# A graph layer with a routed mixture of experts: 104 expert units moved, in pairs, in between the steps over the adjacency matrix

## The reference, cut to what matters

```python
def gnn(z, dist, W, B):                      # z: 8192 x 128, dist (adj): 8192 x 8192
    msg = z @ W + B
    sens = exp(-(1.0 / dist - 1.0) ** 2 / (2 * 0.5 * 0.5))
    weights = where(dist < 1.0, sens, 0.0)
    return weights @ msg

def ffn(x, gate_w, gate_b, w1, b1, w2, b2, gamma, beta):      # 16 experts, 2 for each row
    topk_vals, topk_idx = top_k(x @ gate_w + gate_b, 2)
    topk_w = softmax(topk_vals)
    h = relu(einsum("bsh,ehf->bsef", x, w1) + b1)             # 128 -> 256
    expert_out = einsum("bsef,efh->bseh", h, w2) + b2         # 256 -> 128
    y = x + sum(topk_w[..., None] * take(expert_out, topk_idx))
    return layernorm(y) * gamma + beta

x = x + gnn(layernorm(x), adj, W, B)
x = x + ffn(layernorm(x))
```

## Time and profile before

| what | value |
|---|---|
| median of 3 runs | 1704.23 us (1702.94 to 1705.1) |
| profiled execution, span from first to last instruction | 1823.2 us |
| adjacency loop in it | about 25 to 1433 us |
| tail in it | about 1433 to 1823 us |
| busy: TensorE, ScalarE, VectorE, GpSimd | 1624.7, 1565.7, 1499.7, 463.6 us |

### The profile page before, as it was taken

How to read it: one execution, slowest core, us unless ns; L and a number is a source line. 1 busy time by engine, 2 the same in 40 slices (tenths; PEclk the granted TensorE clock), 3 DMA queues, 4 the chain that set the end, 5 groups by cost and what they waited for, 6 DMA issues and landing times.

```text
span 1823.2 us, 24195 instructions
## 1 busy us (share of the span) xinstructions
PE 1624.7 (89%) x8178; PEld 1073.6 (59%) x8178; DVE 1499.7 (82%) x2298; ACT 1565.7 (86%) x1502; POOL 463.6 (25%) x342
## 2 busy tenths in 40 slices
PE   4999999999999999999999999999999987384720
PEld 3666666666666666666666656666666786373620
DVE  7999998989899999999999989999998443153464
ACT  5899999999999999999999999999999664253531
POOL 0001223131314040407132231313140213535342
PEclk9999999999999999999999999999999999696765
DMA  9559867676767676776776676787673244343431
GB/s 313 158 160 290 235 199 215 195 217 193 214 195 212 196 212 198 220 213 202 210 202 209 199 210 199 209 247 208 202 206 121 80 124 143 87 141 97 129 110 50
DMA packets 216792, 338.22 MB, mean 186 GB/s; under 512 B 18080, under 2 KB 74144, under 8 KB 216544
## 3 DMA queue, kind: packets, MB, share of 16 engines
q1 hardware_dynamic: 208368, 319.62, 59.8%
q0 software_dynamic: 8304, 17.06, 3.1%
HBM read 303.07 MB, written 33.55 MB: 185 GB/s over the span
## 4 chain that ended last, share of the span: by engine, by line
PE 84%; DVE 6%; another core or an unknown queue 5%; issue 3%; ACT 1%; DMA 1%; DVEq 0%; SPq 0%; ACTq 0%
PE acc L1118 48%; PE tp L1137 24%; PE tp L1164 4%; PE tp L1192 3%; PE acc L1192 2%; DVE chunk L654 1%; PE tp L1153 1%; DVE stats L666 1%; DVE chunk L660 1%; DVE chunk L1004 1%; PE misc L1094 1%; ACT chunk L613 1%; DVE msg L729 1%; DMA xs<-in_x_dram 1%
## 5 line engine op out<-in xcount | busy, mean ns | idle before, releaser
L1118 PE MATMUL acc<-wT,msg 128*128 128x512 f32 x2048 | 976.0, 599 | 0.0
L527 ACT ACTIVATE wT<-tp 128x1024 f32<-128x1024 f32 x512 | 761.0, 1674 | 14.0 <-PE tp L1137 12.4
L521 ACT ACTIVATE chunk<-chunk 128x2048 f32<-128x2048 f32 x256 | 655.3, 2560 | 0.1
L660 DVE SCALAR_TENSOR_TENSOR chunk<-chunk 128x2048 f32<-128x2048 f32 x256 | 584.8, 2284 | 54.7 <-ACT chunk L521 54.1
L1137 PEld LDWEIGHTS tp<-ident,chunk 128*128 128x128 f32 x4096 | 478.7, 141 | 223.2 <-issue 221.5
L654 DVE SCALAR_TENSOR_TENSOR chunk<-chunk 128x2048 f32<-128x2048 f32 x256 | 583.5, 2280 | 1.9 <-DMA chunk<-in_adj_dram 1.9
L1137 PE MATMUL tp<-ident,chunk 128*128 128x128 f32 x4096 | 534.3, 274 | 0.0
L516 ACT ACTIVATE chunk<-chunk 128x4096 f32<-128x4096 f32 x118 | 511.0, 4331 | 0.0
L1118 PEld LDWEIGHTS acc<-wT,msg 128*128 128x128 f32 x2048 | 349.1, 190 | 258.3 <-issue 245.8
L457 POOL TENSOR_TENSOR pool_carrier<-pool_carrier 1x1 f32<-1x1 f32 x32 | 43.7, 1365 | 951.5 <-DVE row_now L845 825.9
L476 POOL DMA_INDIRECT rows_in<-y,row_now x128 | 216.7, 1693 | 40.4 <-issue 40.4
(11 more groups left out here) (121 smaller groups left out, 794.7 us busy)
## 6 DMA issues: line engine op xcount, KB each, us to landing
chunk<-in_adj_dram SPq DMA_DIRECT2D x256, 1024.0 KB, 5.4
chunk<-rows_in SPq DMA_DIRECT2D x118, 64.0 KB
rows_out<-chunk SPq DMA_DIRECT2D x59, 128.0 KB
chunk<-rows_in SPq DMA_DIRECT2D x35, 128.0 KB
rows_out<-chunk SPq DMA_DIRECT2D x17, 256.0 KB
y_kept<-y SPq DMA_DIRECT2D x16, 256.0 KB, 6.1
chunk<-y_kept SPq DMA_DIRECT2D x16, 256.0 KB
out_dram<-chunk SPq DMA_DIRECT2D x16, 256.0 KB
```

The costliest lines, as they stand in the source:

```text
L521: act.activation(slot(c), slot(c), ACT.Exp, scale=-1.0).then_inc(inverted, 1)
L527: act.activation(wT[:, (g * PPG + m) % WSLOTS, :], tp[(g * PPG + m) % TSLOTS][:, :], ACT.Exp, scale=-2.0).then_inc(weighted, 1)
L660: dve.scalar_tensor_tensor(out=slot(c), in0=slot(c), scalar=2.0, in1=slot(c), op0=ALU.subtract, op1=ALU.mult).then_inc(squared, 1)
L1118: ins = pe.matmul(acc[:, :], msg[:, n, :], wT[:, (g * PPG + m) % WSLOTS, k * ROWS:(k + 1) * ROWS], start=(n == 0), stop=(n == 2 * PPG - 1))
```

## The change

- Units are always 128 rows; batches are 7, 5, 3 and 1 groups with 72, 55, 39 and 23 units, 189 in all.
- 52 pairs of units (all 36 pairs of the first batch and 16 of the second) run inside the loop in slots behind steps 279, 283, ... A slot does three things for three different pairs, one after the other on TensorE: second layer of pair p - 2, first layer of pair p - 1, transposes of pair p. A slot takes a place in the rotation of the three `tp` banks, so the steps behind it find one bank fewer. ScalarE's part stands behind `weigh` and `invert` at m % 4 = 3, VectorE's (`add_pair_bias`) ahead of the mask of the next step, SyncE loads rows 7 steps ahead of the slot and the first layers one step ahead of it.
- First layers live in DRAM (`first_layers`) until the loop's end; SyncE loads them by pair, and all of them at step 503.
- Tables are made one slot a step from the 26th step of the group after the batch's last.
- Groups 0 to 4 are gathered and combined in the loop (`gather_early`, `early_slot`, from steps 436, 461, 471, 493, 503), wholly on VectorE and GpSimd; these gathers stand on GpSimd between a group's `guess` and its scatter.
- The tail has 85 units, 11 combines starting at iterations 16, 27, 51, 62, 73, 84, 95, 106, 117, 128 and 139 of 152, the gate of group 15 one slot an iteration, the third batch's table at iterations 0 to 10 (its first slots still in the loop) and the fourth's at 26 to 42.

```diff
-    BATCHES = (7, 5, 4)
-    TILES = (1, 2, 1)
...
+    BATCHES = (7, 5, 3, 1)
...
+    UNITS = [K * n * TB + E - 1 for n in BATCHES]
+    UNITS[0] += UNITS[0] % 2
...
+    SLOT_EVERY = 4
+    PAIR_FIRST = [0, UNITS[0] // 2]
+    SECOND_PAIRS = 16
+    NP = PAIR_FIRST[1] + SECOND_PAIRS
+    NE = 2 * NP
+    AT_STEP = [(FIRST[b + 1] + 1) * PPG + 23 for b in range(2)]
+    FIRST_STEP = AT_STEP[0]
+    GRID_OF = [p if p < PAIR_FIRST[1] else (AT_STEP[1] - AT_STEP[0]) // SLOT_EVERY + p - PAIR_FIRST[1] for p in range(NP)]
+    assert GRID_OF[PAIR_FIRST[1]] >= PAIR_FIRST[1] + 2
+    GRID = sorted({t + d for t in GRID_OF for d in range(3)})
+    SLOT_STEP = [FIRST_STEP + SLOT_EVERY * t for t in GRID]
...
+    SLOT_AFTER = {step: n for n, step in enumerate(SLOT_STEP)}
...
+    def place(step):
+        return step + sum(at < step for at in SLOT_STEP)
...
+        COMBINE_FROM = (16, 51, 0, 0)
...
+            for g in range(FIRST[b], FIRST[b + 1]):
+                if g in LATE:
+                    at = max(COMBINE_FROM[b], TAIL0[b + 1] + 8)
+                    starts[g] = max(at, starts[g - 1] + COMBINE_LONG) if starts else at
+        LAST = starts[GROUPS - 1] + COMBINE_LONG + 2
...
+    EARLY_AT = (436, 461, 471, 493, 503)
+    EARLY_GATE = (12, 13, 13, 14, 14)
+    EARLY = len(EARLY_AT)
+    EARLY_SLOTS = 8
...
+            def load_pair(p):
+                if p in PAIR_FIRST:
+                    batch_there(pair_batch(p))
+                if p in PAIR_FIRST or p % PAIRS_AT_ONCE == 0:
+                    take_rows(2 * p, 2 * pairs_until(p))
+                if p >= 3:
+                    sp.wait_ge(turned, slot_place(TURN_SLOT[p - 3]) + 1)
+                for h in range(2):
+                    sp.dma_start(pair_in[:, p % 3, h, :],
+                                 rows_in[bass.ds(unit_rows[2 * p + h], P), :]).then_inc(pair_rows[p % 3], 16)
...
+            def load_pair_weights(p):
...
+                    sp.wait_ge(weighted, WSLOTS + slot_place(HIDDEN_SLOT[p - 2]) + 1)
+                for h in range(2):
+                    sp.dma_start(pair_w[:, p % 2, h, :],
+                                 first_layers[bass.ds(unit_experts[2 * p + h], 1), :, :].rearrange("a p f -> p (a f)")
+                                 ).then_inc(pair_weights[p % 2], 16)
...
+                    if s == SLOT_STEP[OUT_SLOT[p]] + 3:
+                        store_pair(p)
+                    if s == SLOT_STEP[TURN_SLOT[p]] - 7:
+                        load_pair(p)
+                    if s == SLOT_STEP[TURN_SLOT[p]] - 1:
+                        load_pair_weights(p)
+                for h in range(EARLY):
+                    if s == EARLY_AT[h] - 6:
+                        load_early(h)
+                    if s == EARLY_AT[h] + 9:
+                        store_early(h)
...
+            def gather_early(h):
+                last_carried()
+                if h == 0:
+                    results_there(0)
+                    pool.wait_ge(idx_ready, 1)
+                else:
+                    pool.wait_ge(early_free, h)
+                carry()
+                gather(h, 0, early_back, early_rows)
...
+                if h == 0 or g == FIRST[b]:
+                    results_there(b)
+                    pool.wait_ge(idx_ready, b + 1)
+                if h >= BACK:
+                    pool.wait_ge(back_free, h - BACK + 1)
+                carry()
...
+            for g in range(GROUPS):
+                guess(g)
+                for h in range(EARLY):
+                    if EARLY_GATE[h] == g:
+                        gather_early(h)
+                        guess_early(h)
+                if g == GROUPS - 1:
+                    for late in range(EARLY, FIRST[1]):
+                        gather_late(late)
+                scatter(g)
+            for g in range(FIRST[1], GROUPS):
+                gather_late(g)
...
+                act.wait_ge(turned, place(s) + 1)
+                act.wait_ge(added, s + 1)
+                act.activation(wT[:, s % WSLOTS, :], tp[place(s) % TSLOTS][:, :], ACT.Exp, scale=-2.0).then_inc(weighted, 1)
...
+            def pair_slot(n):
+                hid, turned_rows, _ = pair_bank(n)
+                act.wait_ge(turned, slot_place(n) + 1)
+                if n in TURN_SLOT:
+                    ins = act.activation(pair_rT[:, :], turned_rows, ACT.Copy)
+                if n in HIDDEN_SLOT:
+                    p = HIDDEN_SLOT.index(n)
+                    for h in range(2):
+                        for t in range(FT):
+                            i = h * FT + t
+                            ins = act.activation(pair_hT[:, i * P:(i + 1) * P], hid[:, i * P:(i + 1) * P], ACT.Relu,
+                                                 bias=pair_w[:, p % 2, h, F + t:F + t + 1])
+                if n not in TURN_SLOT and n not in HIDDEN_SLOT:
+                    ins = act.activation(act_carrier[:, :], eps[0:1, :], ACT.Copy)
+                ins.then_inc(weighted, 1)
...
+            def add_pair_bias(n):
...
+                if p >= 2:
+                    dve.wait_ge(pair_stored[p % 2], p // 2 * 16)
+                dve.wait_ge(weighted, WSLOTS + slot_place(n) + 1)
+                for h in range(2):
+                    ins = dve.tensor_tensor(pair_out[:, p % 2, h, :], pair_bank(n)[2][:, h * D:(h + 1) * D],
+                                            blobs[:, bass.ds(experts[2 * p + h], 1), B2:B2 + D].rearrange("p a d -> p (a d)"), ALU.add)
+                ins.then_inc(pair_added, 1)
...
+                z, shares = early_z[:, h % 2, :, :], rows(share, h)
+                if m == 0:
+                    dve.wait_ge(early_in[h % 2], (h // 2 + 1) * 16)
+                    dve.wait_ge(early_rows, (h + 1) * KB * 16)
...
@@ -949,6 +1227,9 @@
                     if g and m == BEHIND - 1:
                         gate_sum(g - 1)
                     c, k = divmod(m, PAIRS)
+                    s = g * PPG + m
+                    if s - 1 in SLOT_AFTER and SLOT_AFTER[s - 1] in OUT_SLOT:
+                        add_pair_bias(SLOT_AFTER[s - 1])
...
+            def pair_slot(n):
+                hid, turned_rows, results = pair_bank(n)
...
+                    if p in PAIR_FIRST or p % PAIRS_AT_ONCE == 0:
+                        take_second_layers(2 * p, 2 * pairs_until(p))
+                    pe.wait_ge(weighted, WSLOTS + slot_place(HIDDEN_SLOT[p]) + 1)
+                    for h in range(2):
+                        for t in range(FT):
+                            ins = pe.matmul(results[:, h * D:(h + 1) * D], pair_hT[:, (h * FT + t) * P:(h * FT + t + 1) * P],
+                                            second_layer(2 * p + h, t), start=(t == 0), stop=(t == FT - 1))
+                if n in HIDDEN_SLOT:
+                    p = HIDDEN_SLOT.index(n)
+                    pe.wait_ge(pair_weights[p % 2], (p // 2 + 1) * 2 * 16)
+                    pe.wait_ge(weighted, WSLOTS + slot_place(TURN_SLOT[p]) + 1)
+                    for h in range(2):
+                        for t in range(FT):
+                            i = h * FT + t
+                            ins = pe.matmul(hid[:, i * P:(i + 1) * P], pair_w[:, p % 2, h, t * P:(t + 1) * P],
+                                            pair_rT[:, h * P:(h + 1) * P], start=True, stop=True)
+                if n in TURN_SLOT:
+                    p = TURN_SLOT.index(n)
+                    pe.wait_ge(pair_rows[p % 3], (p // 3 + 1) * 2 * 16)
+                    for h in range(2):
+                        ins = pe.transpose(turned_rows[:, h * P:(h + 1) * P], pair_in[:, p % 3, h, :], ident[:, :])
+                ins.then_inc(turned, 1)
...
-                        pe.wait_ge(weighted, WSLOTS + s + 1 - TSLOTS)
+                        bank_free(place(s))
```

621 lines of the change are left out of this document (377 added, 244 removed).

## The result

| what | before | changed |
|---|---|---|
| median of the timed runs | 1704.23 us | 1738.34 us (1736.0 to 1739.37) |
| ratio, 95% interval | | 1.0199 (1.0183 to 1.0215) |
| recorded span | 1823.2 us, once more 1702.5 us | 1736.6 us |

The change makes the kernel 34 us slower. 1711 was forecast. 1738 lies outside the forecast's own range (1695 to 1730); the wide range (1665 to 1745) holds it only because it was drawn up to rival C (1740), whose mechanism turned out wrong. The direction was forecast, the size was not: +34 us instead of +7.

A forecast was written before the change was run, and what follows sets the result against it. ScalarE was taken to bound the loop (10.75 us per four steps, TensorE close behind); nothing was full in the tail. 1704 + 115 (loop) - 108 (tail) = 1711 us, own range 1695 to 1730, wide range 1665 to 1745.

The forecast's parts named there:

- rival C: Loop: TensorE, ScalarE and VectorE wait for one another in a ring, 0.5 us lost in each of 58 periods; 1740, chance 0.15.
- The holes: Tail: 125 us of waits while GpSimd issues, taken to belong to the recorded execution and hardly to the timed ones.
- Rival B: Tail: the recorded waits are in timed runs too; five gathers leaving the tail take 37 us more along; 1674, chance 0.15.
- The slots' price and the new bound: Loop: 2.00 us of TensorE a slot, 104 for 52 pairs; TensorE becomes the bound at 12.6 us a period.
- The slack of 0.17 us a period: Loop: TensorE's spare time per four steps, given back in 58 periods over steps 279 to 511: -10 us.
- VectorE's new wait: Loop: bias adds wait for ScalarE's slot, mask and logarithm follow; 1.6 us of cover, VectorE comes back in time.
- The early combines: Loop: five combines, 5 us past the cover and 10 of gather waits; 18 together with 3 for the second batch's table.
- Rival A: Loop: no wait of the early combines reaches TensorE; loop +97, tail -116, 1685; chance 0.2.
- Registers: TensorE, VectorE and SyncE load up to 16 expert numbers eight times: +3 us in the loop.
- rival D: Loop: the engine waits out 16 register reads in each loading slot, 23 us more; 1734, chance 0.05.
- The tail: Behind the loop: 85 units at 1.00 us, 11 combines, ending at 157 us against 265: -108, bounds -116 to -98.
- The Trainium skill's explanation: Recorded waits: the block taking the trace's records can stall an engine when an internal FIFO fills; no run yet showed it.

The follow-up runs named there:

- Experiments 4, 5 and 6: Each against the changed kernel: a second hidden-layer copy per slot on ScalarE, 1746.9 us; bias adds behind the mask, 1735.8 us; slots two steps earlier, 1729.5 us.
- experiment 8: Changed kernel with TensorE and VectorE taking expert 0 in every pair slot instead of loading expert numbers into registers: 1736.6 us.
- Experiment 1: Changed kernel with the first batch's table operations spread over more steps: 1735.9 us.
- experiment 3: Changed kernel with no combine in the loop, all 16 in the tail: 1761.0 us.
- experiment 10: Changed kernel with slots two steps earlier, first table spread, early combines later and 17 second-batch pairs: 1732.6 us.
- Experiment 7: Changed kernel with the second batch's 16 pairs left in the tail, only the first batch's 36 in the loop: 1757.2 us.
- place 21: Changed kernel with the slots behind steps 277 + 4t instead of 279 + 4t: 1729.5 us.

## Why the prediction was right, and where it was wrong

- **The holes belong to the recording: right.** The second recording of the kernel before has none, and the changed kernel's span equals its timed runs. The sum was rightly made against a tail of 271 us (269.8 in the clean recording). That the changed kernel's recording would have such holes too (1790) was wrong: they don't come with a block of eight gathers, of which it has 16 as well. Rival B (1674) had nothing under it. Two sums were off by a little: the tail's own terms (144 + 11.2) give 155 where 157 was written, and the recorded span's give 1794 where 1790 was.
- **The slots' price and the new bound: right.** 2.00 us a slot, 12.37 a period, TensorE full, ScalarE with 0.2 us of idle time.
- **The slack of 0.17 us a period: there, but not given back (-10 forecast).** From step 276 to 436, 72.0 of slots made the loop 72.2 longer. The step that failed is the part on VectorE's new wait: "1.6 us of cover" was worked out for the mask and the logarithm alone. What else is queued behind the adds is the gate, and TensorE waits for a piece of it once a group (0.75 us), at two more places less. Experiments 4, 5 and 6 show it from three sides: the longer slot on ScalarE adds 0.5 us to just these periods, the adds behind the mask give 0.9 us back in one of them, and the other place gives all of it. With the 3 us for registers, of which 1 was there, these terms were 7 us too low.
- **The first batch's table: left out.** It was weighed for the second batch only (3 us). That the first batch's now stands one slot a step, where it had been spread with a stride of up to five, costs 6.6 us ahead of any slot, 1.7 of them by the clock behind one wait (experiment 8). The second batch's table, priced at 3, stands at steps 410 to 426 and cost 0.8 at most there (the period from step 416 takes 13.88 us, 13.05 in the other groups). VectorE had 0.25 us a period to spare before the slots (9.1 + 1.4 of 10.75), and four operations of 1.3 us and three of 1.0 fell into four periods. Experiment 1 shows that GpSimd, starved meanwhile, is a good part of it.
- **The early combines: the right mechanism, mis-sized.** "The first early gather can start only when pair 35 is stored" is what happened (1294 us, wanted at 1309, there at 1316.7). 15 us were forecast (18 with the second table); steps 436 to 511 show 26.0. All five combines waited, not three. Two things were missing. A gather in the loop takes 16 to 17.5 us in the changed kernel, and 13 to 26 in the other ones, not always the 15.7 of a scatter; and what TensorE waits for is again a piece of the gate behind VectorE's wait, so there is no cover of its own. And a wait of this length costs more than itself, since the next step can run at half the clock (below). 25.3 of these 26 us go with the combines (experiment 3). Rival A (1685) falls with them: the first `early_z` had 7.40 us of idle time ahead of it.
- **Registers: right; rival D wrong.** By the rule of the Trainium skill ("Runtime: NRT & Kernel Launch", Instruction fetch mechanics), 200 ns for each register, the loads would have been worth 26 us, an estimate. The trace does not agree: their absence moved the slots by 1.1 us.
- **The tail, -108 forecast, -102.6 measured.** The step that failed is 85 units at 1.00 us: they took 112 us, where the sum, with some waits in it, had the last at 103. The 1.00 is right for units alone, not for units beside a combine, the gate and a table on VectorE; 6.8 us of the difference are waits for VectorE, the rest is only partly traced. The rest of the sum held: the last multiplies began 41.8 us behind the last unit (41 forecast), the span ended 11.2 us later. What the tail gained can be told by GpSimd alone: its unbroken row of gathers begins 55.4 us behind the last step instead of 92.4 (37.0), has nine gathers in 94.2 us instead of 16 in 170.0 (75.8), and VectorE ends 23.2 us behind it instead of 13.0 (-10.2): 102.6.
- **Rival C gave nearly the measured time (1740), and is wrong.** It said that each of 58 periods loses 0.5 us. They lose 0.15 on average (102.0 against 100.8 in eight), in two or three of eight, and not through a ring: the short ones have no idle time on TensorE. That the time came within 2 us of its 1740, and inside the stated range, is luck. A price that fits the total says nothing for its mechanism; the profile by steps does.

The sum again, with what was measured: 104.0 of slots, +0.2 in place of -10 + 3, +6.6 in place of nothing, +26.0 in place of 18 (3 of it for a table that stands elsewhere), -102.6 in place of -108: 34.2 against a forecast of 7.

What stays open: 5 us of the tail in experiment 10, and 11 to 12 us of the 112 that the tail's units take. Whether a kernel with early combines and fewer slots in the loop could win was not tried to its end. Experiment 7 speaks against it: the second batch's pairs are not the ones to leave out, and steps 436 to 511 grew by 46.6 us with the five combines and no pairs, as much as the five cost in the tail (46.8, experiment 3).

## What to carry to other kernels

When a wait is put into an in-order queue, list everything behind it until the next point at which another engine takes something from this queue, small operations too: here 1.6 us of cover for the large ones stood beside none for a gate sum of 0.57 us. A step that is placed by its number, and waits for a slow engine that keeps its own pace, gives back what the steps around it gain: of 32 us of work taken out of the loop there only 11 came back. And when two kernels differ by 1 or 2 us behind a wait of TensorE, look at the granted clock before looking for a cause in the edit. Record the kernel before twice when its recorded span is not its timed one.

## What the runs showed of the hardware

**A TensorE that stood can come back at half its clock.** The windows around the first early combine (start:end, length, busy us of each engine, granted clock, DMA) show the granted clock at 1.00 before, and 0.50 (the lower of its two levels, 1.2 GHz) in the step behind a wait of 8.45 us:

```profile
1290.00:1311.00 21.00, 21.00 (x104) 13.32 (x103) 19.34 (x27) 20.67 (x14) 15.61 (x6) 1.00 0.84 251
...
1320.90:1326.20 5.30, 5.24 (x14) 3.10 (x15) 5.30 (x11) 2.82 (x2) 0.00 (x0) 0.50 0.36 81
```

The products of that step took 3.62 us instead of 1.88. A wait of 3.80 us at 1428 was followed by 0.61. So 8.45 us of waiting lengthened these four steps by 11.3 (22.1 against 10.8 in experiment 3, which has the same slots and no combine). In all 14 recordings, from 100 us on, every wait of TensorE of 5 us or more was followed by a mean clock of 0.50 to 0.63 over the next 4 us. Behind shorter ones it differs: eight kernels here wait 2.15 us for `y` at the same step, and seven of them show 0.57 to 0.65 behind it, "no registers" 1.00; behind two waits of 3.80 us "table spread" shows 0.50 and 1.00.

**GpSimd stands until VectorE's large passes end.** The eight gathers of a group take 9.8 to 10.3 us in the changed kernel's tail and 16 to 17.5 in its loop, with the same bytes. The tile's own view (min/median/max in ns):

```profile
L633 POOL DMA_INDIRECT early_back<-rows_out,row_back x40: 940/1890/3232, 1299.3 to 1542.2; - x40
```

An operation on one number took 5.15 us at 1294.00, where it takes 0.18 in the tail. It is worst where VectorE has no gaps, as at the first batch's table. The changed kernel's GpSimd there:

```profile
747.90 10.81 POOL L673 DMA_INDIRECT rows_in<-y,row_now  x1 [0.30 <-issue]
...
766.79 9.41 POOL L621 TENSOR_TENSOR rs<-spread,minus_half 128x4 f32<-128x4 f32 x1
```

A group later they took 1.94 and 2.93 us. What GpSimd waits for shows where one small operation, `spread`, begins under a pass and where it does not. The changed kernel's VectorE and GpSimd, then GpSimd at place 21:

```profile
1062.87 2.26 DVE L864 SCALAR_TENSOR_TENSOR chunk<-chunk 128x2048 f32<-128x2048 f32 x1
...
1063.12 2.10 POOL L619 TENSOR_SCALAR spread<-mv_now 128x4 f32<-128x4 f32 x1 [19.92 <-DVE mv_now L883]
```

```profile
1058.07 0.23 POOL L619 TENSOR_SCALAR spread<-mv_now 128x4 f32<-128x4 f32 x1 [11.17 <-DVE mv_now L883]
```

The first ends 0.09 us behind the mask (1065.22 against 1065.13), the second has no pass beside it. In the 14 recordings the 190 `spread` that overlap a mask or a square take 1.4 to 11.9 us, and the 34 that overlap none 0.2 to 0.5. The 11.90 us of experiment 1 span five passes in a row and end 0.10 us behind the last.

The passes `mask` and `square` have both inputs in SBUF. The Trainium skill ("GPSIMD Engine Reference", section 1, Specifications) names contention of GpSimd with VectorE instructions that have two SBUF inputs; the trace agrees with it, with 2.10 us beside a pass and 0.23 us without.

**Recordings can carry waits of their own.** 119 us in one recording of the kernel before, none in the next, nor in the changed kernel's or the eleven others. The Trainium skill's explanation, quoted ahead of the result, is neither shown nor excluded by this.
